# Splitting catch-up and second-pass matmuls into two of 64 columns, and scaling half of the output on the vector engine

## What is computed

```python
deg0 = clip(sum(adj, 1) + 1, 1); z = concat([X, (adj @ X + X) / deg0]) @ W0 + b
x = layernorm(x + relu(z) / max(norm(relu(z)), 1e-12))
deg1 = sum(adj, 1);  data = concat([x, adj @ x / (deg1 + 1)])
x = layernorm(x + data @ W1.T)
```

## Time and profile before

| | us |
|---|---|
| median of three runs (778.16 to 779.37) | 778.35 |
| the profiled execution, its device time | 778.61 |
| its span, first to last instruction | 776.7 |
| PE busy | 662.5 (85%) |
| DVE busy | 710.8 (92%) |
| ACT busy | 619.5 (80%) |
| last HBM read of `adj` lands | about 680 |

### The profile page before, as it was taken

One profiled execution on the slowest core, in us unless ns is written; L12 is line 12 of the kernel. 1 busy time (PEld: TensorE's weight loads), 2 busy tenths in 40 slices (PEclk: granted clock), 3 DMA queues, 4 the chain that ended last, 5 costly groups with the idle time before them and its releaser, 6 DMA issues.

```text
span 776.7 us, 28012 instructions
## 1 busy us (share of the span) xinstructions
PE 662.5 (85%) x11173; PEld 610.1 (79%) x11173; DVE 710.8 (92%) x2703; ACT 619.5 (80%) x848; POOL 211.1 (27%) x302
## 2 busy tenths in 40 slices
PE   1457777878788888989899999999999999999992
PEld 0357677878677787878798989989998989988992
DVE  4699988999999999999999999999999999988894
ACT  4879798999989898989898988887888988840037
POOL 2225433535333332424313030211102020201024
PEclk9978897989999999999999999999999999999997
DMA  9999999999999999999999999999999999800004
GB/s 302 386 420 420 416 410 420 420 419 419 417 420 421 402 420 404 418 416 415 413 402 418 381 420 372 400 360 408 381 398 386 395 383 387 349 2 3 3 21 93
DMA packets 46125, 274.55 MB, mean 353 GB/s; under 512 B 12647, under 2 KB 12711, under 8 KB 13223
## 3 DMA queue, kind: packets, MB, share of 16 engines
q1 hardware_dynamic: 45184, 270.55, 87.0%
q0 software_dynamic: 576, 2.10, 0.8%
q10 hardware_dynamic: 230, 0.07, 0.0%
HBM read 270.60 MB, written 2.10 MB: 351 GB/s over the span
## 4 chain that ended last, share of the span: by engine, by line
DVE 31%; PE 27%; DMA 12%; issue 12%; ACT 10%; POOL 7%; ACTq 0%; DVEq 0%; SPq 0%; POOLq 0%
PE s_ps L367 13%; DMA a_in<-in_adj 9%; DVE e L766 9%; ACT junk L557 7%; DVE t_sb L773 6%; POOL small L1119 6%; PE u_ps L385 4%; PE p_ps L353 3%; DMA xl<-in_x 3%; DVE q_sb L839 2%; DVE y_sb L833 2%; DVE u_sb L773 2%; DVE a_in L773 1%; PE z_ps L431 1%; PE p_ps L442 1%
## 5 line engine op out<-in xcount | busy, mean ns | idle before, releaser
L557 ACT ACTIVATE junk<-a_in 128x2048 uint8<-128x2048 uint16 x256 | 489.6, 1919 | 3.1 <-DMA a_in<-in_adj 3.0
L367 PE MATMUL s_ps<-xh,t_sb 128*128 128x129 f16 x4096 | 377.9, 247 | 22.9 <-DVE t_sb L773 20.2
L367 PEld LDWEIGHTS s_ps<-xh,t_sb 128*128 128x128 fp8e4 x4096 | 306.2, 100 | 50.5 <-DVE t_sb L773 24.7
L766 DVE TENSOR_SCALAR e<-a_in 128x2048 fp8e4<-128x2048 f32 x256 | 310.7, 1224 | 7.8 <-DMA a_in<-in_adj 6.9
L1127 POOL COPY store<-pk 128x32 uint32<-128x32 uint32 (+1 forms) x250 | 130.2, 562 | 312.0 <-ACT pk L566 312.0
L353 PE MATMUL p_ps<-pow_bf,e 128*128 128x16 bf16 x4096 | 141.8, 170 | 62.7 <-DVE e L766 58.9
L353 PEld LDWEIGHTS p_ps<-pow_bf,e 128*128 128x128 fp8e4 x4096 | 128.9, 96 | 79.2 <-DVE e L766 72.9
L773 DVE TENSOR_SCALAR t_sb<-pk 128x128 uint32<-128x128 uint32 x1024 | 150.8, 222 | 5.3 <-ACT pk L566 4.8
L1119 POOL TENSOR_TENSOR small<-small,minus_half 128x4 f32<-128x4 f32 x32 | 74.6, 2332 | 203.9 <-DVE small L827 162.5
L385 PE MATMUL u_ps<-xh,u_sb 128*128 128x128 f16 x1488 | 99.2, 218 | 0.0
L385 PEld LDWEIGHTS u_ps<-xh,u_sb 128*128 128x128 fp8e4 x1488 | 88.9, 97 | 1.2
(11 more groups left out here) (110 smaller groups left out, 486.9 us busy)
## 6 DMA issues: line engine op xcount, KB each, us to landing
a_in<-in_adj SPq DMA_DIRECT2D x256, 1024.0 KB, 10.3
xl<-in_x POOLq DMA_DIRECT2D x4, 512.0 KB, 16.1
out_h<-e SPq DMA_DIRECT2D x8, 256.0 KB, 2.6
b_sb<-in_L_gnn_b ACTq DMA_DIRECT2D x3, 0.2 KB
w_sb<-in_L_gnn_W ACTq DMA_DIRECT2D x1, 32.0 KB
w_raw<-in_L_gnn_W ACTq DMA_DIRECT2D x1, 32.0 KB
```

What stands on the lines that cost most here:

```text
L367: last = nc.tensor.matmul(s_ps[:, n % 2, at:GW], t_sb[:, b, :], xh[:, b, at:GW], start=(b == 0), stop=False)
L557: nc.scalar.activation(junk[:, t % 2, :], halves[t % R], ACT.Copy, scale=1.0 / 128, accum_out=half_sum[:, n, c:c + 1]).then_inc(s_half, 1)
L766: nc.vector.tensor_scalar(e8[:, c, :], a_in[:, t % R, :], 1.0, None, ALU.is_equal, saturate=False).then_inc(s_e, 1)
```

## The change

1. `catch_up` and the second tail pass (j from 8) issue, for each weight block, two matmuls of 64 columns in place of one of 128: the high and the low columns of `xh`, both into the same 64 PSUM columns, so that PE adds the two parts. The accumulation goes over 16 matmuls instead of 8.
2. `add_piece` and, in the second pass, `add_tail` have one DVE add instead of two.
3. Output groups 4 to 7 are scaled by one DVE instruction each (`scale_rows`), not by eight of ACT; they have their own semaphore `s_o_dve`, and the wait for the output buffer (`s_out`) moves from ACT to DVE. `NA` is 4.
4. The last group's squares and their sum are taken by eight DVE instructions (`last_variance`), not by ACT and a DVE reduce.
5. DVE's list in the second pass: from g = 4 on `variance(g - 1)` stands ahead of `add_tail(8 + g)`, and from g = 6 on `scale_rows(g - 2)` between them.

```diff
             for g in range(NV):
-                sp.wait_ge(s_o, g + 1)
+                if g < NA:
+                    sp.wait_ge(s_o, g + 1)
+                else:
+                    sp.wait_ge(s_o_dve, g - NA + 1)
...
-                for r in (range(half), range(half, r1 - r0))[part]:
+                for r in (range(half), range(half, r1 - r0))[half_of]:
                     for b in range(W):
-                        last = nc.tensor.matmul(u_rows[:, r, :], u_sb[:, r * W + b, :],
-                                                xh[:, low(q - 1) + b, 0:HP], start=(b == 0), stop=(b == W - 1))
+                        for part in range(2):
+                            last = nc.tensor.matmul(u_rows[:, r, 0:F], u_sb[:, r * W + b, :],
+                                                    xh[:, low(q - 1) + b, part * F:(part + 1) * F],
+                                                    start=(b + part == 0), stop=(b + part == W))
...
-                        last = nc.tensor.matmul(v_ps[j % 3][:, r, :], v_sb[:, j % VR, r * W + b, :],
-                                                xh[:, at + b, 0:HP], start=(b == 0), stop=(b == W - 1))
+                        if j < NV:
...
+                            continue
+                        for part in range(2):
+                            last = nc.tensor.matmul(v_ps[j % 3][:, r, 0:F], v_sb[:, j % VR, r * W + b, :],
+                                                    xh[:, at + b, part * F:(part + 1) * F],
+                                                    start=(b + part == 0), stop=(b + part == W))
...
-            for g in range(NV + 1):
-                if g < NV:
-                    squares(g)
-                if g:
+            for g in range(NV - 1):
+                squares(g)
+                if 1 <= g <= NA:
                     finish(g - 1)
...
-                link(nc.vector.tensor_tensor(rows, u_rows[:, 0:r1 - r0, 0:F], rows, ALU.add))
-                nc.vector.tensor_tensor(rows, u_rows[:, 0:r1 - r0, F:HP], rows, ALU.add).then_inc(s_uadd, 1)
+                nc.vector.tensor_tensor(rows, u_rows[:, 0:r1 - r0, 0:F], rows, ALU.add).then_inc(s_uadd, 1)
...
+            def last_variance():
+
+                rows = slice(NB - TG, NB)
+                dve.wait_ge(s_vadd, 2 * NV)
+                dve.wait_ge(s_fvar, NV - 4)
+                for n in range(NB - TG, NB):
+                    ins = nc.vector.scalar_tensor_tensor(out=sqf[:, (NV - 1) % 4, n % TG, :], in0=acc[:, n, :], scalar=1.0,
+                                                         in1=acc[:, n, :], op0=ALU.mult, op1=ALU.mult,
+                                                         accum_out=fvar[:, 1, n:n + 1])
+                link(ins)
...
+            def scale_rows(g):
+
+                rows = slice(g * TG, (g + 1) * TG)
+                dve.wait_ge(s_froot, g + 1)
+                dve.wait_ge(s_out[g % 4], 16)
+                nc.vector.tensor_tensor(o_sb[:, g % 4, :, :], acc[:, rows, :], bc(fvar[:, 1, rows], TG),
+                                        ALU.mult).then_inc(s_o_dve, 1)
...
             for g in range(NV):
+                if g >= 4:
+                    variance(g - 1)
+                if g >= NA + 2:
+                    scale_rows(g - 2)
                 add_tail(NV + g)
-                if g + 12 < 2 * NV:
+                if g < 4:
                     unpack_tail(g + 12)
-                if g:
+                if 1 <= g < 4:
                     variance(g - 1)
-            variance(NV - 1)
+            last_variance()
+            scale_rows(NV - 2)
+            scale_rows(NV - 1)
```

More of the change, by code:

```diff
@@ L38 @@
 TG = 8
+NA = 4
 NV = NB // TG
@@ L232, in gnn_kernel @@
         s_o = sem("s_o")
+        s_o_dve = sem("s_o_dve")
         s_out = [sem(f"s_out{i}") for i in range(4)]
@@ L373, in sum_quarter, with catch_up @@
                     last.then_inc(s_sum, 1)
-            def catch_up(n, part):
+            def catch_up(n, half_of):
                 q, (r0, r1) = seg(n), piece(n)
-                if part == 0:
+                if half_of == 0:
                     pe.wait_ge(s_u, turn(n) + 1)
@@ L441, in tail_sums @@
                     for b in range(W):
-                        last = nc.tensor.matmul(v_ps[j % 3][:, r, :], v_sb[:, j % VR, r * W + b, :],
-                                                xh[:, at + b, 0:HP], start=(b == 0), stop=(b == W - 1))
+                        if j < NV:
+                            last = nc.tensor.matmul(v_ps[j % 3][:, r, :], v_sb[:, j % VR, r * W + b, :],
+                                                    xh[:, at + b, 0:HP], start=(b == 0), stop=(b == W - 1))
+                            continue
[3 more added lines that the diff above has]
+                                                    start=(b + part == 0), stop=(b + part == W))
                 last.then_inc(s_vps, 1)
@@ L621, in finish @@
                 act.wait_ge(s_froot, g + 1)
-                if g >= 4:
-                    act.wait_ge(s_out[g % 4], 16)
                 for k in range(TG):
@@ L898, in add_tail @@
                 rows = acc[:, (j % NV) * TG:(j % NV + 1) * TG, :]
-                link(nc.vector.tensor_tensor(rows, v_ps[j % 3][:, :, 0:F], rows, ALU.add))
-                nc.vector.tensor_tensor(rows, v_ps[j % 3][:, :, F:HP], rows, ALU.add).then_inc(s_vadd, 1)
+                ins = nc.vector.tensor_tensor(rows, v_ps[j % 3][:, :, 0:F], rows, ALU.add)
+                if j < NV:
+                    link(ins)
+                    ins = nc.vector.tensor_tensor(rows, v_ps[j % 3][:, :, F:HP], rows, ALU.add)
+                ins.then_inc(s_vadd, 1)
             def variance(g):
@@ L908, in variance @@
                                                in1=fvar[:, 0, rows], op0=ALU.mult, op1=ALU.add).then_inc(s_fvar, 1)
+            def last_variance():
[6 more added lines that the diff above has]
+                                                         accum_out=fvar[:, 1, n:n + 1])
+                link(ins)
+                nc.vector.scalar_tensor_tensor(out=fvar[:, 1, rows], in0=fvar[:, 1, rows], scalar=1.0 / F,
+                                               in1=fvar[:, 0, rows], op0=ALU.mult, op1=ALU.add).then_inc(s_fvar, 1)
+            def scale_rows(g):
[4 more added lines that the diff above has]
+                                        ALU.mult).then_inc(s_o_dve, 1)
             def verdict():
```

## The result

The changed kernel takes 773.63 us (median of four runs, 772.99 to 774.17) where the kernel before takes 778.62 on the same chip: ratio 0.9935, 95% interval 0.9918 to 0.9952: a gain of 0.65%, small but clear of the noise. The forecast was 767.5, so less than half of the gain came. The profiled execution takes 773.52 us (before 778.61), with a span of 771.7 (before 776.7).

A forecast was written before the change was run, and what follows sets the result against it. Stream bounds blocks 12 to 19, PE from block 44, with stream, DVE and PE limits close together. Loop 7.5 us plus second pass 3.3 made 10.8 off 778.61: 767.8, for the median 767.5; range 761.5 to 777.5.

The forecast's parts named there:

- Bound of blocks 12 to 19: the stream: Loop, blocks 12 to 19: the HBM stream is the bound, 10.0 us a block, so DVE's relief gains nothing.
- Blocks 20 to 35, 4.0 us: Loop: DVE's relief gains 4.0 of the 5.7 us over the stream's 160.0; ends 1.0 and 5.7.
- Blocks 36 to 43, 2.0 us: Loop: three limits within 1.5%; gain 2.0 of the 4.8 us over the stream's 80.0; ends 0 and 4.8.
- Blocks 44 to 51 and from 52 on, 1.0 and 0.5 us: PE-bound loop end: 1.8 and 1.4 us of waits taken back, 0.8 and 0.9 paid for pairs.
- The price of a pair: 57.9 ns forecast: PE: a half of 64 columns costs 29.0 ns, a pair 57.9, 2.3 more than one of 128 columns.
- Rivals 1 (dear halves): PE's matmuls: a pair could cost 76.2 ns, making the program slower, 791.0 us; chance 0.10.
- 3 (the floor): PE's matmuls: halves run at the floor, 50.0 ns a pair, giving 760.2 us; chance 0.12.
- Instruction fetch, nothing: DMA queue: 4000 more instructions to fetch cost nothing; without the stream's room from block 36 on, 0.9 us.
- The second pass, 3.3 us: Tail: last scaling ends at 769.1 against 772.43, gaining 3.3 us; ends 1.5 and 4.3.
- The span ends 4.3 us later, which I leave as it is: After the last scaling: output DMA and flag take 4.3 us, unchanged.
- Rival 2: Loop: PE's waits are chunk hand-overs, so DVE's relief buys nothing; only the tail gains, 777.4 us; chance 0.08.
- The signs named: Forecast wrong if blocks 20 to 43 stay below 410 GB/s despite DVE's falling share, or second-pass DVE waits for PE.

The follow-up runs named there:

- experiments 6: Changed kernel with ACT's sums over 1536 of each chunk's 2048 entries and the check's flag held at zero; 773.43 us, 0.9927.
- 9: Changed kernel with the flag's cast ahead of the last scaling and ACT's copies of h and g one step later; 773.82 us, 0.9926.
- experiment 3: Kernel before with one catch-up add instead of two, matmuls still 128 columns, low columns' product left out of the result; 772.70 us, 0.9921.
- 10: Changed kernel with the flag's cast early and DVE's `low_part` and `begin_acc` moved behind the next block's first compare; 772.30 us, 0.9918.
- experiments 4: Kernel before with catch-up in 64-column pairs, eight high then eight low into separate PSUM columns, both adds kept; 781.09 us, 1.0023.
- experiment 12: Changed kernel with flag cast early and `low_part` in the next block, catch-up's eight high halves before its eight low, same PSUM columns; 771.51 us, 0.9908.
- Experiment 8: Changed kernel with DVE's cast of the check's flag put ahead of its last scaling; 772.71 us, 0.9912.
- Experiments 1: Kernel before with only the loop's part of the change: catch-up in pairs and a single `add_piece` add; 776.23 us, 0.9961.
- 2: Changed kernel with the catch-up put back to 128 columns and two adds, leaving only the tail's part; 776.43 us, 0.9965.
- experiment 11: Kernel before with DVE's `low_part` and `begin_acc` moved behind the next block's first compare; 776.60 us, 0.9970.

## Why the prediction was wrong

The sign, the second pass and the mechanism in PE's waits were right. The size was wrong: 5.0 us for 10.8. By its own steps:

- **Bound of blocks 12 to 19: the stream.** Right, 80.0 us in both. But the pace read from it, "10.0 us for a block", is wrong, and it carries the next term: the first chunks of blocks 12 and 20 land 81.9 us apart before the change (81.6 to 82.1 in all kernels). The compares took only 80.0 because DVE made up a lag of 3.7 us down to 1.7.
- **Blocks 20 to 35, 4.0 us: wrong, and the largest miss.** The step that failed was "DVE falls from 159.6 to 153.6, 96% of the stream's 160.0, which is what the first stretch ran at without loss". Its ends were 1.0 and 5.7 and the truth, nothing, lay outside. The term in it that was wrong is the stream's 160.0: the stream needs 164.4 to 164.6 us for these blocks in every kernel, with its queue at 100% of the 16 DMA engines. So not 5.7 us were to be had but 1.1, and the other 4.6 were the stream's own, which no DVE time touches. The earlier trace rows had the sign, a DMA share of 1.01 in the second stretch as in the first. DVE's share did fall (154.9 us busy), and since it had no one to free it waited, for chunks and for the end of layer 0's chain. Short ACT sums, ACT's copy of h and the pairs are not the cause (experiments 6, 9, 3). The 1.1 us come only when the small steps at the end of a block no longer stand ahead of a compare (10, 164.4 us).
- **Blocks 36 to 43, 2.0 us: right**, 2.5. PE's waits for DVE fell from 5.7 to 1.5 and the rate rose from 405 to 413. The size is in part luck: it was set as a share of 4.8 us over a stream of 80.0. The stream needs 82.2 here (the landings of blocks 36 and 44 after the change, 82.5 before it), so 2.5 us were over it, and the change took them all.
- **Blocks 44 to 51 and from 52 on, 1.0 and 0.5 us: mis-sized.** The mechanism was right twice: the waits went, and the pairs cost. Without the pairs, experiment 3 gains 1.6 us in blocks 44 to 51 and 1.4 from there to the second pass (182.3 to 180.9), against the 1.8 and 1.4 taken back in the forecast. The term that was mis-sized is what the pairs take: not 0.8 + 0.9 but 2.9 together, since a pair costs 3.8 ns more, not 2.3. Of 3.0 us, 0.15 is left.
- **The price of a pair: 57.9 ns forecast, 59.7 measured.** The half of 29.0 ns is the median; the mean has 0.9 more, of which 0.65 is the order of the halves (29.2 in experiments 4 and 12). The Trainium skill's rule (page "TensorE: Matmul & The Clock Gate", section "Back-to-back issue gap") makes it 64/2.4 + 2.5 = 29.2 ns: experiment 12 agrees, the changed kernel's order lies above it. Rivals 1 (dear halves) and 3 (the floor) are refuted by the same rows.
- **Instruction fetch, nothing: right.** The queue has 105 packets for 90, and 0.9% of the engines.
- **The second pass, 3.3 us: right**, 3.25. Variance 2 ends 11.35 us after the first add (forecast 11.3), and PE is ahead of DVE at each step. The steps up to the last root run some 0.15 us ahead of the forecast, the squares and their sum take the time forecast, and the root on POOL takes 2.02 us where 1.66 was forecast; so the last scaling ends 27.6 us after the first add, not 27.5. That root is no chance: the last three roots take 2.02 us in each of the eight kernels that scale groups 4 to 7 on DVE, and 1.64 in each of the six that scale them on ACT. Each of these three starts while DVE is scaling. Timeline of that group:

```profile
763.50 0.17 DVE L932 SCALAR_TENSOR_TENSOR fvar<-fvar 128x8 f32<-128x8 f32 x1
...
763.75 2.02 POOL L1173 TENSOR_TENSOR fvar<-fvar,minus_half 128x8 f32<-128x8 f32 x1 [0.68 <-DVE fvar L932]
...
765.80 0.69 DVE L940 TENSOR_TENSOR e<-xl,fvar 128x512 f32<-128x512 f32 x1 [1.53 <-POOL fvar L1173]
```

- **"The span ends 4.3 us later, which I leave as it is": wrong**, 5.2. Moving the last scaling to DVE put the cast of the flag behind it in DVE's order. Before, the cast ran at 768.58, ahead of ACT's last scaling at 770.41 (the earlier trace rows has the scaling), so PE read the flag while the output was still being made. Now it runs after it, and PE's own finish ends the program. Experiment 8 takes back 0.5 of the 0.9; the other 0.4 is in the landing of the output, 3.3 us from its issue where it took 2.9 before, not explained.
- **Rival 2** (relief buys nothing in the loop) had the nearer truth for the loop outside blocks 36 to 43, with 0.08 of the chance, and for other reasons than its own: in blocks 20 to 35 it was the stream, from block 44 on the price of the pairs. Its reason, that PE's waits are hand-overs which no DVE time shortens, is refuted; they shrank from 5.7 to 1.5 us in blocks 36 to 43 and from 4.3 to none behind them.
- **The signs named.** That "the stream stays below 410 GB/s in blocks 20 to 43" could not have shown the miss: the rate was 414 in blocks 20 to 35 already, and stayed at 413. It counts all bytes moved, and it hid that chunks landed at 408 GB/s (67.1 MB in 164.6 us). DVE did not stand waiting for PE in the second pass, as forecast.

## What to carry to other kernels

A busy engine's relief is worth at most what the engine loses others, and its busy share does not say that. Before pricing relief beside a stream from HBM, read when the same chunks land, not when an engine starts on them: a stretch cut at compares holds the change of the engine's lag as well, and here it made a stream of 10.3 us a block look like one of 10.0. Then list what the relieved engine itself waits for in the stretch, since freed time flows into those waits first. Where the relieved engine is paid for by another that is about to become the bound, price both sides together, with means over hundreds of instructions and not a median of a few. And when the last piece of work moves to another engine, look at everything that stood behind it in that engine's order, down to one-element casts whose readers must still finish.

## What the runs showed of the hardware beside that

- Two matmuls of 64 columns with the same 128 x 128 fp8 weights loaded twice stand 29.7 to 29.9 ns apart; eight with different weights in a row 29.1 to 29.2. Accumulating into PSUM columns that the matmul before wrote costs nothing.
- From DVE's cast of the flag at 766.41 to the row in which PE finishes, 771.5, pass 5.1 us, in experiment 8 from 764.28 to 769.3 5.1, before from 768.58 to 773.7 5.1, in the other kernels 4.6 to 5.3: one engine's reading of a flag and branch at the end of the program. The branch alone takes 3.9 us in these three.
- Six of the 64 chunks of blocks 20 to 35 land some 3.4 us after the one before, the others at most 2.6 us after it, in all fourteen kernels; the first two of these gaps begin at 227 and 255 us in each. Before the change each of the twelve such gaps from 170 to 480 us holds a packet of the instruction queue q14, of which there are 20 in that time; after it 11 of 12 do. That is a coincidence no run tested.
- POOL's copies into `store` became slower where DVE had one add less in the loop. The group on the page of the kernel before, and after (mean ns of one is the second number behind the bar):

```profile
L1127 POOL COPY store<-pk 128x32 uint32<-128x32 uint32 (+1 forms) x250 | 130.2, 562 | 312.0 <-ACT pk L566 312.0
```

```profile
L1166 POOL COPY store<-pk 128x32 uint32<-128x32 uint32 (+1 forms) x250 | 215.0, 901 | 229.7 <-ACT pk L579 229.7
```

Experiments 1 and 3 (904 and 894 ns) have it too, 2 and 4 (559 and 505) do not, so it goes with the single add and not with the pairs; but experiment 11, with both adds and `low_part` moved, has 673, so the add is not all of it. No engine is seen waiting for a copy in the changed kernel, so it cost nothing there; why a copy should take longer beside a less busy DVE no run explains.
